# The Q projection of two pairs of images at once, one half of its output features per step

## The reference

```python
h = tokens(x, W, b, cls_token, pos_enc)              # 64 x 37 x 256
h = concatenate([h, txt], axis=1)                    # 64 x 114 x 256
n = layernorm(h)
Q = elu(n @ Wq.T + bq) + 1;  K = elu(n @ Wk.T + bk) + 1;  V = n @ Wv.T + bv
KV = einsum('bshd,bshe->bhde', K, V);  K_sum = K.sum(axis=1)
Z = 1 / (einsum('bshd,bhd->bsh', Q, K_sum) + 1e-6)
h = h + einsum('bshd,bhde,bsh->bshe', Q, KV, Z).reshape(b, s, E) @ Wo.T + bo
x = layernorm(h);  logits = x @ gate_w.T             # top 1 of 8, weight sigmoid(top)
h = h + w_down[e] @ (silu(w_gate[e] xs) * (w_up[e] xs))
```

## Time and profile before

| | |
|---|---|
| median of 3 runs | 467.21 us (466.26 to 467.88) |
| span of the profiled execution | 473.9 us |
| PE busy | 442.8 us, 93% |
| DVE busy | 333.7 us, 70% |
| ACT busy | 265.2 us, 56% |
| POOL busy | 290.3 us, 61% |
| chain that ended last | PE 70%, POOL 11%, issue 10%, DVE 4% |
| stages by the timeline | patch units to 52, pair loop 52.8 to 333, end of routing and experts to 474 |

### The profile page before, as it was taken

How to read it: one execution, slowest core, us unless ns; L and a number is a source line. 1 busy time by engine, 2 the same in 40 slices (tenths; PEclk the granted TensorE clock), 3 DMA queues, 4 the chain that set the end, 5 groups by cost and what they waited for, 6 DMA issues and landing times.

```text
span 473.9 us, 11189 instructions
## 1 busy us (share of the span) xinstructions
PE 442.8 (93%) x3436; PEld 422.2 (89%) x3436; DVE 333.7 (70%) x1115; ACT 265.2 (56%) x640; POOL 290.3 (61%) x662
## 2 busy tenths in 40 slices
PE   4999999999999999999999999999689599999990
PEld 4999999999999999999999999999668488888870
DVE  5568468988888888888888988997755144344440
ACT  6345466766766766766766765665534244444440
POOL 3145223777777777777777777676467456556563
PEclk9999999999999999999999999999989799999996
DMA  8963121323222121133111112068133782221110
GB/s 285 320 211 112 54 59 47 100 76 102 74 82 66 58 74 51 35 95 98 35 50 53 36 48 67 22 168 226 52 110 110 206 259 84 79 79 64 65 71 24
DMA packets 34139, 46.32 MB, mean 98 GB/s; under 512 B 8842, under 2 KB 25856, under 8 KB 34082
## 3 DMA queue, kind: packets, MB, share of 16 engines
q1 hardware_dynamic: 24860, 30.50, 21.7%
q0 software_dynamic: 9216, 15.12, 10.2%
q10 hardware_dynamic: 6, 0.00, 0.0%
HBM read 26.87 MB, written 17.17 MB: 93 GB/s over the span
## 4 chain that ended last, share of the span: by engine, by line
PE 70%; POOL 11%; issue 10%; DVE 4%; another core or an unknown queue 2%; DMA 1%; ACT 1%; POOLq 1%; SPq 0%; DVEq 0%
POOL out L732 11%; PE b_att L1375 7%; PE b_w L1325 6%; PE b_w L1326 6%; PE b_w L1327 6%; PE b_att L1436 6%; PE b_kg L1325 4%; PE b_kg L1326 4%; PE b_kg L1327 4%; PE b_v L1327 3%; PE b_v L1326 3%; PE b_v L1325 3%; PE b_t L1450 2%; PE b_t L1388 2%; PE b_kg L1571 2%
## 5 line engine op out<-in xcount | busy, mean ns | idle before, releaser
L732 POOL DMA_INDIRECT out<-result,rows_all x64 | 62.5, 976 | 43.8 <-issue 35.9
L654 POOL DMA_INDIRECT sorted_rows<-rows,place x64 | 75.6, 1181 | 20.5 <-POOL place L651 10.6
L1571 PE MATMUL b_kg<-wgu,xsT 128*128 x256 | 67.6, 388 | 0.1
L1244 DVE SCALAR_TENSOR_TENSOR act_u<-b_kg,rows_all,silu_g 128x128 f32<-128x128 f32 x64 | 19.5, 346 | 64.3 <-ACT silu_g L911 50.1
L1571 PEld LDWEIGHTS b_kg<-wgu,xsT 128*128 128x128 f32 x256 | 44.8, 195 | 4.1 <-issue 0.2
L827 ACT ACTIVATE q_exp<-b_w,bq_s 128x228 f32<-128x228 f32 x64 | 28.9, 452 | 30.0 <-PE b_w L1327 30.0
L1325 PE MATMUL b_w<-wo_hi,attnT_hi 128*114 128x264 f32 x124 | 40.2, 324 | 0.0
L1325 PE MATMUL b_kg<-wkgv_hi,xnT_hi 128*114 128x264 f32 x128 | 38.7, 303 | 0.7 <-DVE patch_out L982 0.7
L1325 PE MATMUL b_w<-xnT_hi,wq_hi 128*128 128x256 f32 x128 | 38.5, 301 | 0.9 <-DVE logits L1066 0.6
L1375 PE MATMUL b_att<-v_sb,k_sb 114*128 114x136 f32 x256 | 37.4, 289 | 0.0
L1436 PE MATMUL b_att<-kv_sb,qT 128*114 128x136 f32 x256 | 34.9, 279 | 1.9 <-DVE qT L1044 1.9
(11 more groups left out here) (221 smaller groups left out, 1489.5 us busy)
## 6 DMA issues: line engine op xcount, KB each, us to landing
rows_all<-sorted_rows SPq DMA_DIRECT2D x64, 130.0 KB
rows_all<-in_x SPq DMA_DIRECT2D x18, 384.0 KB, 4.5
rows_all<-in_txt SPq DMA_DIRECT2D x32, 154.0 KB
wgu<-in_wgu_in SPq DMA_DIRECT2D x8, 256.0 KB
rows_all<-patch_out SPq DMA_DIRECT2D x48, 36.0 KB
sorted_rows<-tail_rows SPq DMA_DIRECT2D x9, 130.0 KB
sorted_rows<-rows,place POOLq DMA_INDIRECT x64
wdown<-in_wdown_in SPq DMA_DIRECT2D x2, 512.0 KB, 4.3
```

The lines of the kernel that those rows point to most:

```text
L654: G.indirect_dma_start(out=scratch[0:EXPERTS * REGION, :], out_offset=bass.IndirectOffsetOnAxis(ap=place[:, k, b:b + 1], axis=0), in_=rows ...
L732: G.indirect_dma_start(out=out, out_offset=bass.IndirectOffsetOnAxis(ap=rows_all[:, t.n, ID:ID + 1].bitcast(I32), axis=0), in_=result[:, k ...
L1244: last = V.scalar_tensor_tensor(act_u[:, t.slot(4)], b_gu[m.slot(2)][:, up:up + INNER], rows_all[:, t.n, GAIN:GAIN + 1], silu_g[:, t.slot( ...
L1571: last = T.matmul(to, xsT[:, t.slot(6), k, :], wgu[:, bass.ds(e, 1), k, :], start=(k == 0), stop=(k == KC - 1))
```

## The change

The Q projection no longer takes one pair a step. Two pairs form a group (GROUP = 2), and a step takes one half c of the output features for both pairs: 6 matmuls of 456 columns into one bank of b_w, with no zero columns. Half 0 of group 0 comes between the K and V projections of step 0; from there every step i does half i+1. So the tokens must be turned two pairs ahead: `turn_tokens(i + 2)` stands between V projection and output projection, `tokens_low(i + 2)` on VectorE ahead of the residual, and `normalised`, `tokens_high`, `stats_1` and `rstd1_of` are one pair further ahead. The tokens' and qT's buffers hold two groups, q_exp and q_relu one half. ScalarE makes one exp and one relu of 456 elements per step.

```diff
-QW = 256
+GROUP = 2
+QW = GROUP * 2 * TOK
+        def of_pair(ring, p):
+            first = p % GROUP * 2 * TOK
+            return ring[:, p // GROUP % 2, :, first:first + 2 * TOK]
...
@@ scalar @@
+            def queries(h):
+                c = h % KC
+                act.wait_ge(q_done, h + 1)
+                if h >= 1:
+                    act.wait_ge(q_ready, h)
+                S.activation(q_exp[:], b_w[:, c, 0:QW], ACT.Exp, bias=bq_s[:, c:c + 1])
+                S.activation(q_relu[:], b_w[:, c, 0:QW], ACT.Relu, bias=bq_s[:, c:c + 1]).then_inc(q_parts, 1)
...
-                if 0 <= i + 1 < PAIRS:
-                    normalised(i + 1)
+                if 0 <= i + 2 < PAIRS:
+                    normalised(i + 2)
                 if 0 <= i:
                     keys(i)
+                if i == 0:
+                    queries(0)
+                if 0 <= i:
                     values(i)
+                if 0 <= i + 2 < PAIRS:
+                    tokens_high(i + 2)
                 if 0 <= i - 3:
                     centred(i - 3)
                 if 0 <= i - 1:
                     denominators(i - 1)
-                if 0 <= i + 1 < PAIRS:
-                    tokens_high(i + 1)
-                if 0 <= i:
-                    queries(i)
+                if 0 <= i < PAIRS - 1:
+                    queries(i + 1)
@@ vector @@
-                for k in range(2):
-                    V.memset(xnT_hi[:, k, :, 2 * TOK:].bitcast(F32), 0.0)
-                    last = V.memset(xnT_lo[:, k, :, 2 * TOK:].bitcast(F32), 0.0)
-                last.then_inc(s_posb, 1)
...
-                if 0 <= i - 1:
-                    queries(i - 1)
-                if 0 <= i + 2 < PAIRS:
-                    stats_1(i + 2)
+                if 0 <= i:
+                    queries(i)
+                if 0 <= i + 3 < PAIRS:
+                    stats_1(i + 3)
...
+                if 0 <= i + 2 < PAIRS:
+                    tokens_low(i + 2)
                 if 0 <= i - 2:
                     residual(i - 2)
                     gate_logits(i - 2)
                 if 0 <= i - 1:
                     attention(i - 1)
-                if 0 <= i + 1 < PAIRS:
-                    tokens_low(i + 1)
@@ tensor @@
+            def queries(h):
+                g, c = h // KC, h % KC
+                pe.wait_ge(xnT_lo_ready, GROUP * (g + 1))
+                if h >= 3:
+                    pe.wait_ge(logits_ready, h - 2)
+                elif h == 2:
+                    pe.wait_ge(q_parts, 1)
+                w = slice(c * P, (c + 1) * P)
+                for k in range(KC):
+                    last = product(b_w[:, c, 0:QW], (wq_hi[:, k, w], wq_lo[:, k, w]),
+                                   (xnT_hi[:, g % 2, k, :], xnT_lo[:, g % 2, k, :]), k == 0, k == KC - 1)
                 last.then_inc(q_done, 1)
...
                 if 0 <= i:
-                    project(i)
+                    project_keys(i)
+                if i == 0:
+                    queries(0)
+                if 0 <= i:
+                    project_values(i)
+                if 0 <= i + 2 < PAIRS:
+                    turn_tokens(i + 2)
                 if 0 <= i - 2:
                     project_out(i - 2)
                 if 0 <= i - 1:
                     apply(i - 1)
-                if 0 <= i + 1 < PAIRS:
-                    turn_tokens(i + 1)
-                if 0 <= i:
-                    queries(i)
+                if 0 <= i < PAIRS - 1:
+                    queries(i + 1)
...
-                             *range(11, 17), lambda: early_step(-1), 17])
+                             *range(11, 16), lambda: early_step(-2), 16, lambda: early_step(-1), 17])
```

More of the change, by code:

```diff
@@ L708, in _ @@
             bias_parts(slice(D, KGW))
+            step(-3)
             step(-2)
@@ L815, in tokens_high @@
                 act.wait_ge(turn_done, p + 1)
[L816 to L829, removed]
+                if p >= 4:
+                    act.wait_ge(q_done, p - 2)
+                S.copy(of_pair(xnT_hi, p), turned()).then_inc(xnT_hi_ready, 1)
+            def queries(h):
[5 more added lines that the diff above has]
+                S.activation(q_relu[:], b_w[:, c, 0:QW], ACT.Relu, bias=bq_s[:, c:c + 1]).then_inc(q_parts, 1)
             def step(i):
@@ L895, in _ @@
             act.wait_ge(s_small, 16 * SMALL_DMAS)
+            step(-2)
             step(-1)
@@ L1021, in tokens_low @@
                 dve.wait_ge(xnT_hi_ready, p + 1)
-                low(xnT_lo[:, p % 2, :, 0:2 * TOK], turned(), xnT_hi[:, p % 2, :, 0:2 * TOK]).then_inc(xnT_lo_ready, 1)
+                low(of_pair(xnT_lo, p), turned(), of_pair(xnT_hi, p)).then_inc(xnT_lo_ready, 1)
             def attention_low(p):
@@ L1389, in turn_attention, with tokens_of, project_keys @@
                 last.then_inc(turn_attn_done, 1)
-            def project(p):
-                k_, tokens = p % 2, [slice(b * TOK, (b + 1) * TOK) for b in range(2)]
+            def tokens_of(p, b, k):
+                at = slice(b * TOK, (b + 1) * TOK)
+                return of_pair(xnT_hi, p)[:, k, at], of_pair(xnT_lo, p)[:, k, at]
+            def project_keys(p):
                 pe.wait_ge(xnT_lo_ready, p + 1)
@@ L1400, in project, with project_values @@
                     for k in range(KC):
-                        last = product(to, (xnT_hi[:, k_, k, tokens[b]], xnT_lo[:, k_, k, tokens[b]]),
-                                       (wkgv_hi[:, k, 0:KGW], wkgv_lo[:, k, 0:KGW]), k == 0, k == KC - 1)
+                        last = product(to, tokens_of(p, b, k), (wkgv_hi[:, k, 0:KGW], wkgv_lo[:, k, 0:KGW]), k == 0, k == KC - 1)
                 last.then_inc(kg_done, 1)
+            def project_values(p):
                 if p >= 1:
@@ L1408, in project @@
                     for k in range(KC):
-                        last = product(to, (xnT_hi[:, k_, k, tokens[b]], xnT_lo[:, k_, k, tokens[b]]),
-                                       (wkgv_hi[:, k, KGW:], wkgv_lo[:, k, KGW:]), k == 0, k == KC - 1)
+                        last = product(to, tokens_of(p, b, k), (wkgv_hi[:, k, KGW:], wkgv_lo[:, k, KGW:]), k == 0, k == KC - 1)
                 last.then_inc(kvp_done, 1)
@@ L1435, in apply @@
                     for c in range(KC):
-                        last = T.matmul(b_att[0:TOK, b, c * KVW:(c + 1) * KVW], qT[:, c, b * TOK:(b + 1) * TOK],
+                        last = T.matmul(b_att[0:TOK, b, c * KVW:(c + 1) * KVW], of_pair(qT, p)[:, c, b * TOK:(b + 1) * TOK],
                                         kv_sb[:, b, c, :], start=True, stop=True)
@@ L1442, in turn_tokens @@
                 pe.wait_ge(xn_ready, p + 1)
-                if p >= 3:
-                    pe.wait_ge(attnT_lo_ready, p - 2)
+                if p >= 4:
+                    pe.wait_ge(attnT_lo_ready, p - 3)
                 elif p >= 1:
```

49 lines of the change are left out of this document (21 added, 28 removed).

## The result

| | before | after |
|---|---|---|
| median of the runs compared | 467.54 us (466.26 to 468.64) | 481.86 us (481.51 to 482.58) |
| ratio | | 1.0295, 95% interval 1.0259 to 1.0332 |
| span of the profiled execution | 473.9 us | 480.4 us |

The kernel became 14.3 us slower; the forecast was 479.3, 11.8 above the 467.5 of before.

The account below looks back on a forecast made before the run. Balanced: TensorE's list and VectorE's two chains end together, so moving the turning out of the window adds 0.32 us a step. Way in 3.1 plus loop 9.0 gives +12.1 on 467.21: 479.3 us, range 470 to 484.

Parts of the forecast that it names:

- The window: Last output-projection matmul to rank: Q waits for logits until +1.34, rank for the attention product, unmoved at +2.86 us.
- The price of a Q matmul: Q projection in each step: 0.200 us per 456-column matmul, 1.29 for six, against 1.49 before.
- The price of the turning: Four transposes moved between V and output projection: 0.32 us more a step (0.25 to 0.40), 9.0 over 28 steps.
- The way in: Ahead of the loop and in steps 0 and 1: four terms, 3.1 us more, between 1 and 4.
- (b): Step 0 on TensorE: two Q halves run and the turning stays, 5.85 us instead of 4.76, +1.09.
- (c): Step 0 on VectorE: Q's first half and statistics come ahead of K, which TensorE then awaits, +0.65 us.
- (d): Step 1: Q finds the tokens of pair 3 not ready, +0.8 us, less 0.2 for Q, +0.6.
- (a): Ahead of the last patch unit and step 0: second turning 0.32, second pair of statistics 0.46, sum 0.78 us.
- VectorE's cover: Low half (0.54 us) ahead of the residual fits in 0.69 of idle time, with 0.15 over.
- The way out: Behind the loop: last apply's wait for Q's product goes, but the tanh chain holds; nothing taken, bounds 0 and -1.
- The difference between profile and median: Median 467.21 lies 6.7 us below the profiled span of 473.9; carried over whole, from span 486.0 to 479.3.
- The rival: Tail: ScalarE's stall, perhaps from instruction fetch, moves later in its shorter list and is hidden; 471.4 us, chance 0.08.

Follow-up runs that it names:

- the shortened kernel before: The kernel before with 4 of the 12 Q matmuls of a pair left out (low weights times high tokens); 466.48 us, ratio 0.9951.

## Why the prediction was right

**The window, right.** Q was to start at +1.34 behind the logits, and to lie between two chains, with rank unmoved at +2.86. Rank stands at +2.86. Q started at +1.43: a 456-column Q begins 0.14 to 0.15 after the logits in every step from 75 to 325 us of the changed kernel, where the 256-column one began 0.06 after them in the earlier trace rows and 0.05 to 0.06 in the kernel with the turning moved alone. The 0.09 fell into the wait. That the attention product holds rank was read from one late product; the shorter Q of both kernels and the shorter attention chain showed it.

**The price of a Q matmul, right.** 0.200 us was forecast; the steady spacing in the step above is 0.21 (215.72 to 215.93). A Q half is 1.31 us (214.83 until 215.93 + 0.21), not 1.29, against 1.49 before. The Trainium skill, "TensorE: Matmul & The Clock Gate", section "Back-to-back issue gap", gives 131 ns per matmul of 512 columns in a stream; the trace disagrees for these fp32r products. It is nearer to the isolated gap of the same section, N / 2.4 + 2.5 ns, which makes 192.5 ns of 456 columns, an estimate by that page.

**The price of the turning, too small.** This is the term that was off: 0.32 from the earlier trace rows, with 0.40 as the upper bound, and it measured 0.39. I had argued that the new place might be cheaper, since a bf16 matmul follows the transposes and not the slower first fp32r one. But the bf16 one starts 0.39 later instead of 0.32, and the fp32r one behind it starts no faster than before. Over 28 steps that is 2.0 us. The loop took 10.16 more against 9.0; 0.8 less than 28 x 0.39 = 10.9, since the loop of before had a few long steps of its own.

**The way in, near in sum, with one term at half its size.** The sum was 3.1 and measured 3.77. Step 0 took 6.36 against a forecast of 6.50 ((b) and (c)), step 1 7.22 against 7.15 ((d)), each wait with the cause named: K's VectorE product, the tokens of pair 3.

```profile
60.64 1.19 PE L1383 MATMUL b_att<-v_sb,k_sb 114*128 114x136 f32 x8 [0.37 <-DVE k_sb L1059]
...
66.52 0.47 PE L1333 MATMUL b_w<-xnT_hi,wq_hi 128*128 128x456 f32 x1 [0.46 <-DVE xnT_lo L950]
```

(a), ahead of step 0, was put at 0.78, at most 1.32, and reads 1.50 (54.28 against 52.78). A single trace can't judge it: of the kernels with the way in of before, step 0 started at 52.78, 52.68, 50.91 and 51.15, though all four do the same up to there. But the six kernels with the changed way in started it at 53.36 to 54.28, later than any of the four, and the two medians lie 1.6 us apart. So (a) was mis-sized, about 1.6 for 0.78. What share of it is the second turning and what the second statistics stays open.

**VectorE's cover, right.** The low half ahead of the residual was to fit with 0.15 over. The residual starts at +0.32, where it did, with 0.29 idle ahead.

**The way out, right in sum, with a swap inside.** The last apply no longer waits 1.88 us for Q's VectorE product, and it starts 2.25 after pair 31's K-transposed-V instead of 4.03. But it takes 2.13 us instead of 1.15. Before and after, TensorE:

```profile
337.49 1.15 PE L1436 MATMUL b_att<-kv_sb,qT 128*114 128x136 f32 x8 [1.88 <-DVE qT L1044]
```

```profile
347.19 0.19 PE L1366 MATMUL b_att<-chosen,earlier 114*114 114x16 bf16 x1 [1.65 <-DVE attn L1095]
...
349.64 2.13 PE L1449 MATMUL b_att<-kv_sb,qT 128*114 128x136 f32 x8 [0.21 <-DVE place_f L1133]
```

And the stretch of that apply, after (columns as above):

```profile
349.60:352.00 2.40, 2.36 (x10) 2.38 (x11) 1.42 (x6) 2.17 (x6) 0.40 (x4) 0.50 0.00 0
```

The granted clock is 0.50 there, the 1.2 GHz level, after TensorE had stood still for 1.65 us ahead of rank and waited 0.21 ahead of this apply. The missing Q of step 31 is not what decides it: with the turning three pairs ahead that Q is missing too, and the clock stays at 1.00 and the apply at 1.15. In the profiles of all thirteen kernels the clock was down at the last apply in seven of the eight that turn ahead of the output projection in some or all steps, and in none of the five that turn behind apply. The gaps which the turning's place leaves in the loop can't be the whole reason: the eighth kernel, the one with VectorE's order changed, has the same steps of 9.30 us and the same waits of 1.65 and 0.19, and its apply took 1.15. Nor does the clock of before stay up. It falls later, in the expert stage (columns as above):

```profile
349.00:352.70 3.70, 3.70 (x16) 2.73 (x15) 2.14 (x9) 1.85 (x5) 1.99 (x8) 0.54 0.61 211
```

Of the thirteen kernels only before without the copy of the denominators shows no such fall between the loop and the last ten microseconds or so. So the runs show that the moment of the fall differs; what sets it stays open. Neither the earlier start nor the slower apply matters for the end: the low half of pair 31's attention comes 8.82 after the last K-transposed-V against 8.94, as the tanh that holds it was to make it.

**The difference between profile and median: right for the median, wrong for the span.** It was carried over whole, so the stall of the earlier trace rows was taken to belong to the profiled execution. From the last K-transposed-V to the end it was 140.4 us in before's profile, 133.0 in the changed kernel's, and 132.9 in that of the shortened kernel before (462.8 - 329.89), whose expert stage is untouched; none of the other twelve profiles took more than 136.1. The changed kernel's profiled execution was timed at 482.20 us for a span of 480.4. By the same 1.8 us, before's span of 473.9 would be a time of 475.7, above every timed run of it (at most 470.73). So the timed runs of before had no such stall, and nothing was won by its absence after. The span of the changed kernel was forecast at 486.0 and came out at 480.4, since the stall didn't come again.

What the stall was stays open. The rival weighed the fetching of instructions. Before's profile does list transfers of instructions, 28 packets on queue q8 and 29 on q14, but none between 364.9 and 372.5 us, the stretch of both of ScalarE's stalls; the next one comes between 372.5 and 375. That speaks against a fetch as their cause.

So 12.1 was forecast on the 467.2 of before, and 14.3 came: 1.2 in the loop and 0.7 on the way in by the one trace of each kernel; the last 0.4 lies within what two medians differ by.

## What to carry over

In a loop whose engines are balanced, find the window in which TensorE races against the chains beside it. Look for it by starts and not by busy time, and ask of every moved instruction on which side of the window's ends it stood and stands. Work taken out of the window frees nothing until the chain beside it is shortened too, and work put outside it is paid in full, even if it is the same four transposes. Here a wider operand that forced its producer ahead was better paid with one more stage of lead than with a place outside the window: with three pairs of lead and a shorter chain the kernel with the same wide Q is 0.5% faster than before. The shorter chain alone gives 0.3%, and the times don't separate the two.

## What was new about the hardware

- A first fp32r matmul of 456 columns on a just released bank starts 0.14 to 0.15 us after the releasing VectorE instruction ends, one of 256 columns 0.05 to 0.06 (the earlier trace rows and the turning moved alone). The wide one has a second wait, for the tokens' low halves; no run separates that from the width.
- Four 114-column transposes cost 0.32 us ahead of a 256-column fp32r matmul and 0.39 ahead of a bf16 one, on which another fp32r one follows at once. What they cost ahead of a 456-column one no run shows, since the logits released it in every step.
- A VectorE reciprocal of 114x32 straight from PSUM takes 0.36 us, from SBUF 0.35. ScalarE's copy (0.29 and two handovers) only lengthened the chain; what it did besides was to add the 1e-6, which the kernels without it leave out.
- In seven of the eight kernels that turn outside the window the granted clock was 0.50 at the last apply, whose eight matmuls took 2.13 us instead of 1.15. In the other six it was 1.00 there. It fell to 0.50 in five of those six too, but later: in before only in the expert stage.
